# Group whitening of 32 images: Norm's matmul one slot earlier, and the last two images evicted by two engines and stored in six parts by two queues

## The reference

```python
x1 = x.reshape(N, C // G, G, H, W).transpose(0, 2, 1, 3, 4).reshape(N, G, -1)
xc = x1 - x1.mean(-1, keepdims=True)
cov = xc @ xc.transpose(0, 2, 1) / M + EPS * jnp.eye(G)
# decorr = cov ** -0.5 by 10 Newton-Schulz steps
Y, Z = cov / norm(cov), I
for _ in range(10):
    T = 0.5 * (3.0 * I - Z @ Y); Y = Y @ T; Z = T @ Z
decorr = Z / sqrt(norm(cov))
y = weight1 @ decorr @ xc + bias1
```

## Time and profile before

| what | value |
|---|---|
| median of 3 runs | 448.66 us (445.0, 448.66, 482.71) |
| the profiled execution | 441.01 us |
| span from its first to its last instruction | 438.8 us |
| mean granted TensorE clock | 0.954 of full speed |
| PE, DVE, ACT busy | 86%, 73%, 76% of the span |
| moved by DMA | 152.10 MB, mean 347 GB/s |

### The profile page before, as it was taken

One profiled execution on the slowest core, in us unless ns is written; L12 is line 12 of the kernel. 1 busy time (PEld: TensorE's weight loads), 2 busy tenths in 40 slices (PEclk: granted clock), 3 DMA queues, 4 the chain that ended last, 5 costly groups with the idle time before them and its releaser, 6 DMA issues.

```text
span 438.8 us, 16961 instructions
## 1 busy us (share of the span) xinstructions
PE 377.7 (86%) x7360; PEld 262.2 (60%) x7360; DVE 320.2 (73%) x1018; ACT 333.6 (76%) x450; POOL 33.7 (8%) x66
## 2 busy tenths in 40 slices
PE   0768799998999989999999999999999997978750
PEld 0767666675666657656767576675766665743310
DVE  5776878787878878887888887878888887632200
ACT  5873389897889888978989898888788898434660
POOL 0000001010111000000011001000101011110000
PEclk9995989999999999999999999999999999976995
DMA  7999967899999999999999999999999987565997
GB/s 263 418 409 410 411 251 211 217 385 403 383 390 392 380 390 395 403 400 401 383 387 382 407 401 403 410 403 407 402 394 409 387 261 214 133 177 157 255 331 249
DMA packets 29130, 152.10 MB, mean 347 GB/s; under 512 B 3968, under 2 KB 3968, under 8 KB 21120
## 3 DMA queue, kind: packets, MB, share of 16 engines
q1 hardware_dynamic: 22048, 97.92, 60.2%
q0 software_dynamic: 6720, 53.09, 32.7%
q10 hardware_dynamic: 288, 0.01, 0.0%
HBM read 75.51 MB, written 75.50 MB: 344 GB/s over the span
## 4 chain that ended last, share of the span: by engine, by line
PE 70%; DVE 9%; ACT 9%; issue 6%; DMA 2%; SPq 0%; ACTq 0%; DVEq 0%
PE cov_ps L475 30%; PE y_ps L544 25%; PE chain_ps L511 6%; ACT image L251 4%; ACT image L261 4%; DVE transposed L348 2%; DMA image<-x 2%; PE chain_ps L509 2%; PE cov_ps L487 1%; DVE wyz L400 1%; PE chain_ps L517 1%; PE chain_ps L527 1%; DVE folded L408 1%; PE shift_ps L463 1%; PE chain_ps L507 1%
## 5 line engine op out<-in xcount | busy, mean ns | idle before, releaser
L348 DVE STREAM_TRANSPOSE transposed<-image 128x384 f32<-128x384 f32 x384 | 213.5, 570 | 12.2 <-ACT image L251 2.8
L261 ACT ACTIVATE image<-y_ps,y_bias 128x768 f32<-128x768 f32 x192 | 166.9, 893 | 53.3 <-PE y_ps L544 52.8
L475 PE MATMUL cov_ps<-transposed 128*64 128x65 f32 x4608 | 175.7, 229 | 9.3 <-issue 9.3
L544 PE MATMUL y_ps<-image,apply_w 64*64 64x384 f32 x1536 | 176.0, 517 | 3.8 <-issue 2.4
L475 PEld LDWEIGHTS cov_ps<-transposed 128*64 128x64 f32 x4608 | 158.8, 141 | 26.3 <-issue 11.5
L251 ACT ACTIVATE image<-image,shift 128x1152 f32<-128x1152 f32 x128 | 156.1, 1248 | 1.7 <-DMA image<-x 0.6
L544 PEld LDWEIGHTS y_ps<-image,apply_w 64*64 64x64 f32 x1536 | 55.8, 134 | 13.9 <-ACT image L261 7.6
L511 PE MATMUL chain_ps<-wyz,t_mat 64*64 64x96 f32 x256 | 46.9, 264 | 3.4 <-DVE t_mat L396 3.3
L511 PEld LDWEIGHTS chain_ps<-wyz,t_mat 64*64 64x64 f32 x256 | 27.0, 135 | 35.1 <-DVE t_mat L396 29.1
L400 DVE SCALAR_TENSOR_TENSOR wyz<-wyz,chain_ps 64x96 f32<-64x96 f32 x128 | 30.0, 235 | 24.4 <-PE chain_ps L511 24.0
L509 PEld LDWEIGHTS chain_ps<-wyz 64*64 64x64 f32 (+1 forms) x256 | 28.7, 139 | 31.9 <-DVE wyz L400 19.9
(11 more groups left out here) (62 smaller groups left out, 164.2 us busy)
## 6 DMA issues: line engine op xcount, KB each, us to landing
image<-x SPq DMA_DIRECT2D x128, 576.0 KB, 17.2
y<-image POOLq DMA_DIRECT2D x30, 1152.0 KB, 12.0
y<-image SPq DMA_DIRECT2D x32, 576.0 KB, 13.5
y<-image POOLq DMA_DIRECT2D x30, 576.0 KB, 7.9
y<-image SPq DMA_DIRECT2D x1, 1152.0 KB, 7.7
y<-image SPq DMA_DIRECT2D x3, 384.0 KB, 3.9
y<-image SPq DMA_DIRECT2D x6, 192.0 KB, 3.8
b_col<-bias ACTq DMA_DIRECT2D x4, 0.1 KB, 6.4
```

Source lines behind the costliest of these rows:

```text
L261: nc.scalar.activation(xs[n % SLOTS][:, :, STRIP * q:STRIP * (q + 1)], y_ps[:, f % 2, :, 0:STRIP], ACT.Identity, bias=y_bias[:, c % 2, i:i ...
L348: nc.vector.transpose(xt[q][:, TILES // 2 * part:TILES // 2 * (part + 1), 0:CH], xs[n % SLOTS][:, h, at:at + TWELFTH]).then_inc(transposed, 1)
L475: ins = nc.tensor.matmul(cov_ps[rows, n % 2, 0:GRAM], xt[q][:, t, 0:CH], xt[q][:, t, 0:GRAM], start=q == 0 and t < 2, stop=q == IMAGE_PIEC ...
L544: ins = nc.tensor.matmul(y_ps[out_rows, f % 2, h, 0:STRIP], apply_w[rows, c % 2, i].rearrange("p k g -> p (k g)"), xs[n % SLOTS][rows, h, ...
```

## The change

The change has four parts.

1. `NORM`'s matmul on TensorE moves from slot 2 to slot 1, that is from behind strip 0 of pair `c - 2` to ahead of it. The table also moves `NORM`'s six instructions on VectorE from slot 4 to slot 3. `NEXT_0` stays in slot 5.
2. `shift_of(1)` moves from ahead of the first covariance piece to behind it.
3. The strips of the last pair (pair 15, images 30 and 31) are evicted by ScalarE where `f` is even and by VectorE where it is odd, each with a semaphore of its own. TensorE waits for the one that holds the buffer.
4. Each of the last two images is stored in three parts of two strips, so six parts `k`. Of each, SyncE's queue stores the plain piece and the crossed piece from partitions 0 to 63, and ScalarE's queue the crossed piece from partitions 64 to 127. ScalarE issues part `k` behind its eviction of strip `2k + 2`, the last one behind all.

```diff
-PARTS = {IMAGES - 2: 1, IMAGES - 1: 3}
+PARTS, PART = 3, 2
+LAST_PAIR = IMAGES // 2 - 1
-OFFSET_AT, NORM_AT, NORM_OUT_AT, NEXT_0_AT = 0, 2, 4, 5
+OFFSET_AT, NORM_AT, NORM_OUT_AT, NEXT_0_AT = 0, 1, 3, 5
...
+        def wait_part(engine, k):
+            engine.wait_ge(y_read, FLAT * LAST_PAIR + PART // 2 * (k + 1))
+            engine.wait_ge(y_read_dve, PART // 2 * (k + 1))
+
+        def store_part(engine, k, h, rows, channels):
+            n, q = IMAGES - PAIR + k // PARTS, PART * (k % PARTS)
+            cols = slice(STRIP * q, STRIP * (q + PART))
+            engine.dma_start(out_v[n, channels, h, cols], xs[n % SLOTS][rows, h, cols]).then_inc(stored_last, 16)
...
-            for n in range(IMAGES - PAIR, IMAGES):
-                size = IMAGE_PIECES // PARTS[n]
-                for q in range(0, IMAGE_PIECES, size):
-                    store_plain(sp, n, slice(q, q + size), stored_last)
-                    for upper in range(2):
-                        store_crossed(sp, n, slice(q, q + size), upper, stored_last)
+            for k in range(PAIR * PARTS):
+                wait_part(sp, k)
+                store_part(sp, k, 0, slice(0, P), slice(0, P))
+                store_part(sp, k, 1, slice(0, HALF), slice(HALF, P))
...
-                    if exists(before):
+                    if exists(before) and before != LAST_PAIR:
                         output(before, f)
...
                     if exists(c - 2):
                         output(c - 2, 2 * j)
+                    if c - 2 == LAST_PAIR and j > 0:
+                        wait_part(act, j - 1)
+                        store_part(act, j - 1, 1, slice(HALF, P), slice(0, HALF))
...
+            wait_part(act, PAIR * PARTS - 1)
+            store_part(act, PAIR * PARTS - 1, 1, slice(HALF, P), slice(0, HALF))
...
+            dve.wait_ge(offset_dve, PAIRS)
+            for f in range(1, FLAT, 2):
+                i, q = f // IMAGE_PIECES, f % IMAGE_PIECES
+                dve.wait_ge(y_done, FLAT * LAST_PAIR + f + 1)
+                nc.vector.tensor_scalar(xs[(IMAGES - PAIR + i) % SLOTS][:, :, STRIP * q:STRIP * (q + 1)],
+                                        y_ps[:, f % 2, :, 0:STRIP], y_bias[:, LAST_PAIR % 2, i:i + 1], None,
+                                        ALU.add).then_inc(y_read_dve, 1)
...
-                if m >= 2:
+                if c == LAST_PAIR and f >= 2:
+                    if f % 2:
+                        pe.wait_ge(y_read_dve, f // 2)
+                    else:
+                        pe.wait_ge(y_read, FLAT * c + f // 2)
+                elif m >= 2:
                     pe.wait_ge(y_read, m - 1)
...
-            shift_of(1)
...
-                    if j % 3 == 0 and 1 < ahead < IMAGES:
+                    if j % 3 == 0 and ahead < IMAGES:
                         shift_of(ahead)
```

More of the change, by code:

```diff
@@ L163, in whiten @@
         y_read = sem("y_read")
+        y_read_dve = sem("y_read_dve")
         block = ctx.enter_context(nc.Block())
@@ L207, in _ @@
                     load(n - 1 + SLOTS)
-            for n in range(IMAGES - PAIR, IMAGES):
-                size = IMAGE_PIECES // PARTS[n]
-                for q in range(0, IMAGE_PIECES, size):
-                    store_plain(sp, n, slice(q, q + size), stored_last)
-                    for upper in range(2):
-                        store_crossed(sp, n, slice(q, q + size), upper, stored_last)
-            sp.wait_ge(stored_last, 16 * 3 * sum(PARTS.values()))
+            for k in range(PAIR * PARTS):
+                wait_part(sp, k)
+                store_part(sp, k, 0, slice(0, P), slice(0, P))
+                store_part(sp, k, 1, slice(0, HALF), slice(HALF, P))
+            sp.wait_ge(stored_last, 16 * 3 * PAIR * PARTS)
             for n in range(IMAGES - PAIR - SLOTS, IMAGES - PAIR):
@@ L283, in _ @@
             sum_shift(1)
-            for c in range(PAIRS + 3):
+            for c in range(PAIRS + 2):
                 for j in range(ROUNDS):
                     before, f = (c - 2, 2 * j - 1) if j else (c - 3, FLAT - 1)
-                    if exists(before):
+                    if exists(before) and before != LAST_PAIR:
                         output(before, f)
```

## The result

The changed kernel took a median of 459.66 us (458.88 to 465.98 in 4 runs), against 462.67 us for the kernel before beside it (445.0 to 482.71 in 4 runs). Executions that the comparison finds disturbed are left out of its ratio, which leaves three of the changed kernel (458.88 to 460.33) against two of the kernel before (445.0 and 448.66): 1.028, with an interval of 1.017 to 1.039. The predicted time, 451, is too low, and 459.66 lies just above the range's end of 459. The medians of all executions point the other way from the ratio, so how far the kernel scatters by itself is part of the case, and this first comparison alone doesn't say that the change is slower.

A forecast was written before the change was run, and what follows sets the result against it. TensorE was taken to bound the middle, stores of three images the end. Terms -0.9 + 6.9 + 1.1 - 3.0 = +4.1 us gave 445.1 against 441.0 (+0.9%), placed at 451 us between lowest and median runs; range 441 to 459.

The forecast's parts named there:

- the stores: Kernel end: crossed pieces from both partition halves run together in two queues, shortening the end; -3.0 us.
- the stores stay as they are: Rival for the end: halves don't run together, or image 29 blocks an earlier start; tail gives 0, +7.1 us total; chance 0.14.
- VectorE's side of Norm: Middle, pairs 0 to 14: a second transposition ahead of NEXT_0 leaves the root's shadow, 0.46 us each; +6.9 us.
- TensorE's side, middle: Middle: moving NORM's matmul earlier gains nothing, and its wait for L429 is covered by TensorE's idle time; 0.
- Round trip 16: Round trip without transpositions or covariances: strip 0 now stands behind the matmul that waits for L429; +1.1 us.
- The first covariance piece: Start: TensorE does 24 covariance matmuls before its wait for the sum of image 1; -0.9 us.
- The last strips and ScalarE's issues: End: two evicting engines keep the 1.9 us buffer period, and ScalarE's five store issues fit its free time; 0.
- The clock: Rival: the half-level clock seen from 389 to 402 us falls elsewhere or not at all; 4.5 us lower, 440.6; chance 0.09.

The follow-up runs named there:

- cut version: Changed kernel with the stores of images 0 to 27 cut to one of six strips; median 435.64 us, against 423.90 for the kernel before with the same cut.
- the new end alone: Parts 3 and 4 of the change alone on the kernel before: whole, 465.43 us; with the stores of images 0 to 27 cut to one of six strips, 426.13.
- Splitting strictly by side: The cut kernel with two evicting engines, SyncE's queue storing only from partitions 0 to 63, ScalarE's only from 64 to 127; 424.33 us (four parts), 424.12 (six).
- five arrangements of queues and parts: Ends tried in the cut kernel: two queues 425.85 us, image 30 in three parts 424.27, whole new end 426.13, sides in four parts 424.33, in six 424.12.
- the cut kernel: Kernel before with the stores of images 0 to 27 cut to one of six strips; median 423.90 us (422.57 to 425.61, 4 runs).
- Both slots: The cut kernel with NORM's matmul in slot 1 and VectorE's six instructions in slot 3, nothing else changed; median 434.15 us.
- TensorE's alone: The cut kernel with only NORM's matmul moved to slot 1, VectorE's six instructions staying in slot 4; median 427.13 us.
- the end alone: Whole kernel before with only parts 3 and 4 of the change; median 465.43 us, the kernel before beside it 456.47.
- the start alone: Whole kernel before with only shift_of(1) moved behind the first covariance piece; median 466.46 us, the kernel before beside it 456.47.
- six parts by sides: The cut kernel with two evicting engines and six parts of two strips, SyncE's queue storing partitions 0 to 63, ScalarE's 64 to 127; median 424.12 us.
- the middle's split: Whole kernel before, stores of images 0 to 29 split by partition half between SyncE's and GpSimd's queues: 472.06 us, ratio 1.050; with the sides' end 470.13, 1.057.

## Why the prediction was wrong

The step that failed is the stores: "Now the crossed pieces from partitions 0 to 63 and from 64 to 127 lie in two queues and can run together", at T + 23.1 for -3.0 us. The span ended at T + 27.0, 27.2 and 27.2 in the two profiles of the changed kernel and its cut version, at T + 26.15 and 27.1 in the two with the new end alone. With the old end it was T + 26.0 to 26.6 in seven profiles and 27.2 and 27.6 in two. So the term is nothing, or up to 1 us the other way, and the gain of 3 us isn't there.

The runs showed two things in its place. The parts didn't start earlier: up to T + 10 image 29 held the engines, with 1.68 of the 1.90 MB that moved from T + 4 on. And with both queues at work, the halves had 290 GB/s together, the one queue before 279. I had divided all of the upper partitions' bytes by the half rate, as if both halves were always busy. Splitting strictly by side had 326 GB/s in its last 13 us instead of 282, which is the one gain that a trace shows, and still short of 417. So "running both halves together is right", which the prediction drew from the ports, is borne out in a small part only. The rival "the stores stay as they are" names both reasons and describes the result; its price of 0 is right within what the old end scatters by itself. The rule that stands behind that rival, the Trainium skill's DMA: Bandwidth & Descriptors, Rules for kernel authors (disjoint partition halves serialize), did better than my assumption: by it the second queue gains nothing, and five arrangements of queues and parts gained nothing that can be timed. The split by sides shows that halves don't serialize altogether.

The other terms, in the cut kernel, where each can be read without the pauses:

- *VectorE's side of Norm*, predicted +6.9: right. Both slots have 434.15 and TensorE's alone 427.13, so VectorE's part is +7.0 by the medians, to within some 2 us. The traces say it more finely. From the root of pair 2 to that of pair 15, 13 round trips, the rows of all roots are, cut before:

```profile
L267 ACT ACTIVATE col<-chain_ps x14: 148/150/154, 78.1 to 377.9; 64x1 f32<-64x1 f32 x14
```

cut with both slots:

```profile
L267 ACT ACTIVATE col<-chain_ps x14: 150/152/153, 79.5 to 387.1; 64x1 f32<-64x1 f32 x14
```

cut with TensorE's slot alone:

```profile
L267 ACT ACTIVATE col<-chain_ps x14: 147/150/152, 79.5 to 381.4; 64x1 f32<-64x1 f32 x14
```

That is 299.8, 307.6 and 301.9 us. Both slots cost 7.8 more than none: twelve times 0.46, and 2.4 in the last round trip, of which 0.46 is again the transposition and 1.9 the term of round trip 16 below.
- *TensorE's side, middle*, predicted 0: right, 23.20 us a round trip with and without.
- *Round trip 16*, predicted +1.1: mis-sized. The wait came out as predicted (1.17 us); what the term left out is that the clock falls behind it and strip 0 takes 0.75 us longer. The rows above give 301.9 - 299.8 = +2.1, of which 1.9 in the last round trip. In the cut changed kernel it is 1.4 us besides the transposition's 0.46; there the clock fell only in the middle of the two strips (16 matmuls in 2.36 us). The whole kernels don't show this cost: their clock is at its half level there with the old slots too, and from the root of pair 14 to T it took 46.0 to 47.7 us in four traces with the old slots (the kernel before twice, the end alone, the start alone) and 43.6 to 45.8 in four with TensorE's new one. So this term of the cut kernel doesn't carry over.
- *The first covariance piece*, predicted -0.9: the step happened (it starts at 9.05 us after, not 12.97), and root 0 came at 30.2 to 30.7 us in the four profiles with the edit, at 31.1 to 31.6 in fourteen of the sixteen without. By root 1 the lead was gone: 54.4 us with the edit alone, 54.5 in the second profile of the kernel before. The term is about 0. Root 1 varies from 54.4 to 58.6 us over all profiles, and each of them has a stretch at half clock before it.
- *The last strips and ScalarE's issues*, predicted 0: right. VectorE's eviction took 1.02 us, estimated 1.0; the last one ended at T + 12.8, before at T + 12.2.
- *The clock.* In the cut changed kernel's profile the last chain ran at the half clock for 20 us behind a fall at 386.4, and came 7.0 us later to T than in the cut kernel before. Its execution was 440.33 us, the other three 434.79 to 435.94. The fall itself belongs to the change: TensorE's clock fell behind the new wait of 1.3 us in all three profiles of cut kernels with TensorE's new slot, and in none of the seven without. How long it stayed down differed, about 3, 3 and 20 us, for a reason that the traces don't show. The size that I gave it (4.5) is the right order, but I had it as a possible gain.

Between the two profiles of the cut kernels, +17.9 us of span, the parts are -0.9 to root 0, +3.2 to root 1, +5.8 to root 14, +1.9 to root 15, +7.0 to T and +1.0 behind it. Some 8 us of this is the order of the steps (15 x 0.46 and 1.4 at round trip 16). What is left of the +11.7 us between the medians isn't taken apart by any run: the end may hold up to 1 us, and the mean granted clock was 0.952 to 0.965 in the four executions of the cut changed kernel against 0.973 to 0.981, so a part of it is the clock.

Whether the whole kernel is slower by 2% stays open. Cut, the change costs 2.8%. Whole, the two comparisons gave 1.028, from few executions, and 1.015 with an interval that holds 1. Taking all, the changed kernel's 10 runs have a median of 459.66 (450.16 to 473.3), and 54 runs of the kernel before that stood beside others 454.5 (437.75 to 482.71), or 453.2 with the six of its own run (from 431.48): +1.1% and +1.4%. That is near the +0.9% of the forecast, but by luck in part, since the stores' -3.0 wasn't there and round trip 16 and the clock came out differently.

What put the number outside its range was the level. I placed +0.9% on three runs of 445.0 to 482.71, which came to about 447 for the kernel before, where many runs have 453 to 454. The scatter is the pauses. That they go with the DMA traffic is shown, since lowering its share from 1.01 to 0.64 removed them in every cut kernel. That late instruction blocks are what ends them rests on the order of events in the traces, though it is the same at all 84. Whether an edit makes them more frequent (the kernel with only the start changed had 466.46 and 19.6 us of such idle time ahead of its covariances) or whether that was chance stays open, and so does why the split by sides is slower. Also open is what holds the final stores at about 300 GB/s, with the engines' share at 0.92 to 0.95, where 417 were reached for 4 us.

No version beat the kernel before: the best end (six parts by sides) gains 1.0 us in the trace of a cut kernel and nothing in its time. In a whole kernel the sides' end was only tried together with the middle's split, where it ended at T + 26.4 instead of 27.2.

## What to carry to other kernels

A step may be moved earlier only as far as its releaser allows. What counts is what comes to stand behind its wait (here strip 0 of round trip 16) and which work left the shadow of another wait (here one transposition, 0.46 us a pair, +6.9 in all). Two queues don't double a rate because their pieces lie in different halves: ask what the engines are still moving when the new stores are issued, and what rate the halves reach together in a trace. Where a kernel scatters by 20 us, thin out the traffic that makes it scatter, and measure the edits there: +11.7 us was plain with 4 runs, where whole kernels gave 1.015 with an interval that held 1. But a thinned kernel is another kernel: a wait that makes the clock fall there may stand in a stretch that is at half clock anyway in the whole one, so read each part in the traces of both before carrying its cost over.

## What the runs showed of the hardware

- TensorE stood up to 7.4 us with nothing that the profile shows to wait for while the DMA engines were full, and went on 1.2 to 1.6 us behind the landing of a 16 KB block on the instruction queue, at each of 84 pauses of over 1 us behind the first 60 us of ten traces. At a DMA share of 0.64 such pauses were absent in ten traces and runs agreed within 3 to 6 us.
- Issuing a store took 0.35 us on a free queue and 1.7 us on average over SyncE's twelve with data in flight (1.2 over eighteen in another end); ScalarE's took 0.56 to 1.51 us. Landings of 192 KB stretched from 3.8 us to 6.7 and 8.6 us.
- TensorE's clock fell to its half level behind a wait of only 1.3 us in three cut kernels, for about 3, 3 and 20 us.
- The last stores moved 282 GB/s on one queue, 309 on two with pieces of all 128 partitions on one of them, and 326 with each queue kept to its own 64 partitions (the last 13 us of three cut kernels). Pieces of all 128 partitions had reached 417 for 4 us.
- VectorE evicts 128 x 768 float32 from PSUM with a bias in 1.02 us, ScalarE in 0.90.
